# The output's store of a transformer layer on one Trainium2 core, issued by SyncE instead of ScalarE

## The reference

```
q, k, v = x @ wq + bq, x @ wk + bk, x @ wv + bv
attn    = softmax(q k^T / sqrt(16))            # per sequence and head, 128 x 128
out     = (attn v) @ wo + bo
n       = layernorm(x + out) * g1 + be1
y       = n + relu(n @ w1 + b1) @ w2 + b2      # hidden size 512
result  = layernorm(y) * g2 + be2
```

## Time and profile before

| | |
|---|---|
| median of 3 runs | 4191.73 us (4184.59 to 4194.13) |
| the profiled execution | 4193.59 us |
| its span from first to last instruction | 4191.8 us |
| mean granted TensorE clock | 0.992 |
| busy: PE, PEld | 98%, 84% |
| busy: DVE, ACT, POOL | 87%, 83%, 88% |
| DMA issues of the output's store | 256, of 256 KB each |

### The profile page before, as it was taken

The page is one execution under the profiler, slowest core; times in us unless marked ns, Lnnn a source line. Parts: engine busy times, 40 slices in busy tenths (PEclk is TensorE's granted clock), DMA queues, the critical chain, the costliest instruction groups (busy, mean ns, idle before and its releaser), DMA issues.

```text
span 4191.8 us, 150532 instructions
## 1 busy us (share of the span) xinstructions
PE 4090.8 (98%) x49930; PEld 3541.1 (84%) x49930; DVE 3650.1 (87%) x9740; ACT 3494.4 (83%) x5890; POOL 3708.3 (88%) x3864
## 2 busy tenths in 40 slices
PE   6999999999999999999999999999999999999997
PEld 5888888888888888888888888888888888888886
DVE  6888888888888888888888888888888888888885
ACT  4888888888888888888878888888888888888886
POOL 4889998998899999989989889998999998988987
PEclk7999999999999999999999999999999999999999
DMA  7777777777777777777767777777777777777772
GB/s 150 183 179 189 183 185 185 183 188 180 187 181 189 179 188 186 182 185 183 186 173 180 188 180 186 185 182 184 184 190 181 188 182 184 185 182 185 181 187 76
DMA packets 1466634, 755.76 MB, mean 180 GB/s; under 512 B 644736, under 2 KB 1432960, under 8 KB 1465856
## 3 DMA queue, kind: packets, MB, share of 16 engines
q1 hardware_dynamic: 1158672, 605.66, 58.6%
q10 hardware_dynamic: 307184, 140.40, 12.2%
HBM read 202.51 MB, written 134.22 MB: 80 GB/s over the span
## 4 chain that ended last, share of the span: by engine, by line
PE 40%; DVE 18%; issue 12%; ACT 10%; POOL 8%; SPq 5%; DMA 3%; ACTq 3%; DVEq 1%; POOLq 0%
PE bankB L705 6%; DVE max_sb L559 5%; PE bankC L705 5%; PE s_ps L719 5%; POOL rs L332 5%; PE bankC L682 5%; PE oT_ps L746 5%; PE sT_ps L733 5%; PE bankB L682 3%; DMA x_blocks<-in_x 3%; ACT n_sb L459 3%; DVE st L576 3%; PE bankA L759 3%; SPq L247 2%; ACT m_sb L417 2%
## 5 line engine op out<-in xcount | busy, mean ns | idle before, releaser
L559 DVE TENSOR_REDUCE max_sb<-s_ps 128x8 f32<-128x1024 f32 x1024 | 1218.4, 1190 | 7.1 <-PE s_ps L719 5.8
L429 ACT ACTIVATE prob_sb<-sT_ps 128x1024 f32<-128x1024 f32 x1024 | 1046.3, 1022 | 153.3 <-PE sT_ps L733 110.1
L288 POOL TENSOR_TENSOR parts<-rest_sb,parts 128x512 bf16<-128x512 f32 x512 | 584.4, 1163 | 187.4 <-ACT parts L396 177.6
L719 PEld LDWEIGHTS s_ps<-stack 96*128 96x128 bf16 x8192 | 465.1, 98 | 278.5 <-issue 152.9
L719 PE MATMUL s_ps<-stack 96*128 96x128 bf16 x8192 | 641.0, 222 | 25.7 <-DVE max_sb L559 16.3
L459 ACT ACTIVATE n_sb<-z_sb,shift,rs 128x128 f32<-128x128 f32 x1024 | 422.1, 482 | 264.0 <-POOL shift L334 264.0
L733 PE MATMUL sT_ps<-stack 99*128 99x128 bf16 x8192 | 629.0, 219 | 4.3 <-ACT prob_sb L429 4.1
L746 PE MATMUL oT_ps<-prob_sb,v_ones 128*32 128x128 f32 x16384 | 555.1, 276 | 5.0 <-ACT prob_sb L429 3.3
L705 PE MATMUL bankB<-w_sb,h_sb 128*128 128x128 f32 x4096 | 526.9, 282 | 16.7 <-ACT h_sb L408 15.4
L746 PEld LDWEIGHTS oT_ps<-prob_sb,v_ones 128*32 128x32 f32 x16384 | 417.1, 110 | 128.7 <-issue 51.1
L733 PEld LDWEIGHTS sT_ps<-stack 99*128 99x128 bf16 x8192 | 503.9, 98 | 7.1 <-ACT prob_sb L429 5.7
(11 more groups left out here) (75 smaller groups left out, 8401.0 us busy)
## 6 DMA issues: line engine op xcount, KB each, us to landing
stack<-parts SPq DMA_DIRECT2D x3072, 128.0 KB
x_blocks<-in_x SPq DMA_DIRECT2D x1024, 64.0 KB, 2.4
n_mem<-n_sb SPq DMA_DIRECT2D x1024, 64.0 KB
n_blocks<-n_mem SPq DMA_DIRECT2D x256, 256.0 KB, 3.5
out<-out_sb ACTq DMA_DIRECT2D x256, 256.0 KB, 4.1
x_sb<-in_x ACTq DMA_DIRECT2D x255, 256.0 KB, 3.1
stack<-max_parts ACTq DMA_DIRECT2D x768, 8.0 KB
h_sb<-in_L_conv_w SPq DMA_DIRECT2D x1, 256.0 KB, 2.9
```

Source lines behind the costliest of these rows:

```text
L288: pool.tensor_tensor(parts[:, r % 2, 3 * c + LO], rest_sb[:, c], parts[:, r % 2, 3 * c + MID], ALU.subtract).then_inc(lo_split, 1)
L429: act.activation(prob_sb[:, s % 2], sT_ps[:], ACT.Exp, scale=float(D) ** -0.5).then_inc(exp_done, 1)
L559: dve.reduce_max(max_sb[:, (r - lag) % 2, :, s], s_ps[:].rearrange("p (h k) -> p h k", h=H), AX.X).then_inc(max_done, 1)
L719: ins = pe.matmul(s_ps[:, h * P:(h + 1) * P], stack[0:PROD, (r - lag) % 4, 0, h, tok], stack[0:PROD, (r - lag) % 4, 1, h, tok], start=True ...
```

## The change

SP issues the output's store at the end of its step, behind the last stack row, and waits there for `out_ready`. ACT no longer waits for `out_ready` and no longer issues the store. The step's number at which the group r-9 is stored stays the same. SP's `iterate` now runs to lag 9, and ACT's to lag 8.

```
--- before.py
+++ after.py
@@ -261,8 +261,11 @@
                     stack_rows(t, r, 1, HI, hi_split)
                     stack_rows(t, r, 1, MID, mid_split)
                     stack_rows(t, r, 1, LO, lo_split)
-
-            iterate(sp, step, 0, LEAD, LAST, 5)
+                if live(t, r, 9):
+                    sp.wait_ge(out_ready, upto(t, r, 9, plus=1))
+                    sp.dma_start(out_g[t + (r - 9)], out_sb[:, (r - 9) % 2]).then_inc(out_stored[(r - 9) % 2], DMA)
+
+            iterate(sp, step, 0, LEAD, LAST, 9)
             sp.wait_ge(out_stored[(G - 2) % 2], upto_dma(0, G - 2, 0))
             sp.wait_ge(out_stored[(G - 1) % 2], upto_dma(0, G - 1, 0))
 
@@ -435,9 +438,6 @@
                     if (v := upto(t, r, 0)) is not None:
                         act.wait_ge(k_done, v)
                     act.activation(xT_parts[:, HI], xT_sb[:], ACT.Copy).then_inc(xT_hi, 1)
-                if live(t, r, 9):
-                    act.wait_ge(out_ready, upto(t, r, 9, plus=1))
-                    act.dma_start(out_g[t + (r - 9)], out_sb[:, (r - 9) % 2]).then_inc(out_stored[(r - 9) % 2], DMA)
                 exponentials(t, r, 0)
                 if live(t, r, 7):
                     relu(t, r, 7, 2)
@@ -498,7 +498,7 @@
             step(0, 0)
             act.wait_ge(consts_loaded, N_CONST * DMA)
             act.wait_ge(consts_made, N_MADE)
-            iterate(act, step, 1, LEAD, LAST, 9)
+            iterate(act, step, 1, LEAD, LAST, 8)
 
         @block.vector
         def _(dve):
```

## The result

The change is slower. Its median is 4225.06 us (4221.47 to 4228.49, 4 runs) against 4188.16 us (4183.74 to 4194.13, 4 runs) of the kernel before on the same chip: a ratio of 1.0087, 95% interval 1.0070 to 1.0105. The forecast was 4182.2 us in a range of 4173 to 4200, so time and sign were both missed. The profiled execution took 4224.23 us, 30.6 us more than the one before (4193.59).

A forecast was written before the change was run, and what follows sets the result against it. PE was taken as the bound, with a 15.76 us floor against 16.00 us per step. Terms of -10.5 (ACT) and +1 (SP), others 0, gave 4184.1 us profiled, or 4182.2 us against the median; range 4173 to 4200.

The forecast's parts named there:

- the transfer's: DMA engines: 67.1 MB move from ACT's ring to SP's, 0.9 us of all engines per store; costed at nothing.
- a sign of being wrong on the added side: DVE's wait for x_blocks grows, or POOL waits over 20 us in total for the store's DMA before L362.
- The term of SP's issue: SP's queue: 256 added issues of 0.5 us, mostly hidden by SP's idle time before L247; +1 us, bounds 0 and 5.
- The idle time of 320 us: Sign on SP: its wait for n_sb before L247 falls to near 320 us, against 447.7 before.
- ACT's term: ACT's queue: without the store's long issues, PE regains two thirds of its 15.4 us wait before L705; -10.5 us.
- The buffer's term: POOL's L362 rewriting `out_sb`: the store lands 0.6 us early in the mean, and up to 1.2 us lateness goes unseen; 0.
- the rival of late landing: Store queued behind nine stack rows lands too late for POOL's L362: about 4210 us at 6.0 us landing; chance 0.04.
- The stalls did not simply go elsewhere: Rival: long issues hit ACT's other DMAs or PE finds another late partner; 4186 to 4193, likeliest 4189 us; chance 0.38.
- the sign that was named for it: PE's waits for v_ones before L759 grow by what its wait before L705 loses.
- SP falling behind: Rival: store issues of 1.6 us on SP delay stores of n and loads of x; about 4207 us; chance 0.08.

The follow-up runs named there:

- the run with 8 KB beside the store on ACT: Kernel before, its store still on ACT, plus an 8 KB DMA to a scratch buffer on SP behind the last stack row: 4198.6 us, ratio 1.0010.
- the first experiment: Kernel before with the output's store kept on ACT but issued one place later, behind ACT's load of x (L465): 4255.0 us, ratio 1.0148.
- the swap of two blocks: SP's loads of x issued ahead of the stores of n: kernel before 4171.57 us, ratio 0.9941; the change 4162.35 us, ratio 0.9921.

## Why the prediction was wrong

**The step that failed is the transfer's.** It said: "In a step of 16 us there is room. I cost it at nothing in both directions". The runs put the bytes at some 50 us in the new place, against 6 us in the old one. So the move adds 44 us for the transfer, and with the 8 us gained otherwise that is the measured loss of 0.87%. The arithmetic in it was right: 0.9 us of all engines in a step of 16. The fault was to ask whether the engines have room on average, not what stands directly behind the store in time. The answer was in the earlier trace rows and in the words on the kernel: the first of four stores of n follows 1.8 us behind in the mean, then four loads of x, then DVE's transpose, which already waited for x in 29 steps before. A row with 15.1 us of such waits was on hand and was not priced, since I looked at what the store could delay through SP's issue alone. The growth of DVE's wait for x_blocks was named as a sign of being wrong on the added side, and it is the sign that came: 15.1 us became 54.2.

**The term of SP's issue** (+1 us, bounds 0 and 5) was low but within its bounds: about 4 us by the run with 8 KB beside the store on ACT, whose interval is wide. The idle time of 320 us that was forecast for SP came out as 335.7, the issue of 0.5 us as 0.53.

**ACT's term** (-10.5 us) was right in mechanism. PE's wait before L705 fell by 9.4 us, and with 8 KB in both places the move is worth 0.19%, 8 us. In the change the gain is there and is covered by the loss.

**The buffer's term** (0) came out right, with one slip in its working: the landing times are counted from the start of the issue, and the 0.5 us of the issue was added to them once more. The spare time was 1.1 us in the mean and not 0.6, and the rival of late landing was priced too close by the same 0.5.

**The rivals.** The stalls did not simply go elsewhere: PE's waits for v_ones before L759, the sign that was named for it, are 16.4 us against 15.0 before. Part of them did move on ACT, whose idle time by issue before L491 grew by 9.1 us, but PE hardly saw it. SP falling behind was the rival with the right sign, and it named the right victims, the stores of n and the loads of x. But its price came from a longer issue, and its test was SP's idle time under 0.8 us in the mean. That idle time is 335.7 / 255 = 1.3 us and the kernel is slower all the same: the mechanism in it did not happen. The late landing did not happen either: 3.6 us, and POOL waits 7.0 us in ten steps. The Trainium skill's rule on ring order (DMA: Bandwidth & Descriptors, Queues, rings and completion order) was weighed for the store's own landing, where it changed nothing. It can be part of why the stack rows came late when the store stood ahead of them, but no run here shows that; for the loads of x it is not needed, since the store in ACT's ring, a little later in the step, harmed them more. The Trainium skill's statement in the same page's section Issuing engines are not separate DMA queues, that DMAs of all issuers run on the same 16 engines and interleave, agrees with the first experiment: 77.3 us of waits for x against 15.1, from a store in the other ring.

**Where the expected gain went:** off ACT, as planned; paid back about five times over in steps in which the loads of x landed late.

**Open.** How the transfer slows the loads is not settled between their slower issue and their slower transfer, and the traces show both. In the steady part the four loads take 2.23 us to issue in the mean, against 2.18 before, and the last lands 2.43 us behind the end of its issue, against 2.27; in the 19 tight steps it is 2.86 and 2.85. Why an issue gets longer is open, and so is the cause of the long issues that hit both queues. Nor was the number of rows in the store tried apart from its bytes.

## What to carry to other kernels

A DMA that is moved to a queue with idle time takes its bytes along: ask which transfer follows within its time to landing, and whether somebody already waits for that one, however little. Cut the bytes and keep the instruction to tell issue from transfer; one run separated them here. (The rows of the transfer shrink with it; to tell those from bytes takes another run.) And where a late load waits for nothing that is late itself, put it ahead of the DMAs that do wait: here the swap of two blocks gained 0.6% alone and turned the moved store from a loss of 0.9% into part of a gain of 0.8%.

## What was not expected of the hardware

An 8 KB store of 128 rows of 64 bytes is issued in the same 0.53 us as a 256 KB store of 512 rows of 512 bytes (0.529 and 0.531 us on SP, in medians). On ACT it is 0.379 against 0.421. The 8 KB DMA to the scratch buffer, with rows of the same size, took 0.449 on SP, so bytes and rows do not fix the time of an issue here. The bytes that cost 1.2% of the kernel's time do not show in the issue that started them, only in what stands behind it.

The long issues have a companion in time. In the kernel before, 75 of ACT's 78 issues over 0.9 us end within 0.06 us of an SP issue over 0.9 us. Counting such ends on the two queues, those that fall together once, gives 353 moments. Of these 209, or 59%, lie 1.25 to 2.0 us behind the start of a DMA of the kind that the profile calls "instruction", while such stretches are 11% of the time. No run tested whether one causes the other.
